# Attention and channel mix on one core: q stacks in two parts on SyncE, x asked for later, the second projection in idle banks

## The chip, the cores and the metric

One core of a Trainium2 chip runs the whole program. The metric is the device time of one execution in microseconds (us). TensorE is PE in the profile, with PEld for its weight loads; VectorE is DVE, ScalarE is ACT, GpSimd is POOL, SyncE is SP. SPq and ACTq rows are DMA issues on the queues of SyncE and ScalarE.

## The reference

```python
x = layernorm(x + attn(x)); x = layernorm(x + ffn(x))        # x: 1 x 4096 x 256, float32
# attn: 16 heads of 16, 4 groups of k and v, window of 128 keys, causal
scores = einsum('bghqd,bgkd->bghqk', q, k) / sqrt(16);  mask = (i - 128 >= j) | (i < j)
out = softmax(where(mask, -1e9, scores)) @ v;  return out @ Wo + bo
# ffn: x_prev is x one token earlier
r = sigmoid(xr @ W_r.T); k = square(relu(xk @ W_k.T)); return r * (k @ W_v.T)
```

## The kernel before

The 4096 tokens are 32 blocks of 128 (t), four blocks to a superblock (s, eight of them; j is the block's place in its superblock, 0 to 3). All queues are written out by hand: each engine has a function start() and a function step(s, j, ...), called once for each block, and engines meet at semaphores. A step works on several blocks at once: the row maxima of block t+1, the scores, exponentials and masks of block t, the product with v of block t-1, the output projection of t-2, the channel mix of t-3 and t-4, and the store of t-5.

Projections are made by superblock. Each of its three chunks (chunk 0 is k and v, chunks 1 and 2 are q) is projected in float32 by TensorE (`project_chunk`, L876), and split by ScalarE (`high_part`, L492, and `middle_part`, L503), VectorE (`rest_part`, L663) and GpSimd (`low_part`, L378) into three bf16 parts whose sum is the float32 value. Chunks 0 and 1 of superblock s+2 are made in step j=3 of s, chunk 2 in step j=0 of s+1. The parts are written to DRAM (`spill_k` L298, `spill_q` L292) and read back with the six combinations of parts stacked along partitions, 16 rows for each: `stack_k` (L311, L313) into ks, 80 KB each, and `stack_q` (L512) into qs. One superblock's q stack is six transfers of 256 KB, each to 16 partitions, and ks and qs have two buffers, by the superblock's parity (par).

`tile_q` (L680) on VectorE copies a block's queries from qs into q_tiles, two steps ahead of the block: in step j=2 of superblock s it takes the first block of s+1, in j=3 the second. The maxima's products (`max_scores`, L923 and L932) of the next step begin with it. VectorE reduces them (L688), and `turn_max` (L695 to L702) turns the maxima into rows, which SyncE sends to two rows of qs (`max_in`, L321, two transfers of 4 KB) for the score product of the next block (L949).

In the step, SyncE issues in this order: in j=0 `spill_k`, the wait for its landing, six `stack_k`, `max_in`, then `spill_q` twice; in j=1 `max_in`, `load_x(s+2)` (x_t and x_in, 512 KB each); in every step the store of block t-5 last. ScalarE issues the six `stack_q` of superblock s+1 in step j=1, between its exponentials 4 and 5. GpSimd adds bo to the four blocks of x of s+1 in step j=2 (`x_plus_bo`, L372).

In the start, superblock 0 is projected in three banks, superblock 1 in proj_ps alone, one chunk after the other, and its chunk 2 after the second group of block 0's maxima. ScalarE issues the whole q stack of superblock 0 there, and VectorE's first `tile_q` waits for all of it. VectorE waits on s_stack, which counts the six k and the six q transfers of a superblock together.

```python
                if j == 0:
                    dve.wait_ge(s_stack, s * STACKS + STACKS)
```

Of the kernel before, what the change touches and what calls it, by code (L numbers as in the profile page):

```python
# [32 lines left out]
WINDOW = 128  # L33
# [4 lines left out]
SB_BLKS = 4  # L38
# [16 lines left out]
def attention_channel_mix(nc, x_nat, x_feat, w_first, w_rest, out):  # L55
# [25 lines left out]
    with ExitStack() as ctx:  # L81
# [6 lines left out]
        def sem(name):  # L88
            return ctx.enter_context(nc.semaphore(name))
# [85 lines left out]
        s_spill_k = sem("s_spill_k")  # L175
        s_spill_q = sem("s_spill_q")
        s_stack = sem("s_stack")
        s_tiles = sem("s_tiles")
        s_maxsc = sem("s_maxsc")
        s_max = sem("s_max")  # L180
# [93 lines left out]
        def _(sp):  # L274
# [26 lines left out]
            def stack_k(s, par, rep):  # L301
                if rep == 0:

                    sp.wait_ge(s_spill_k, s * 16 + 16)
                    if later(s, 2):

                        sp.wait_ge(s_score, scored(s * SB_BLKS - SB_BLKS - 1, NSCORE - 1))
                    sp.nop(nofuse=True)
                src = k_dram[K_PART[rep]].rearrange("(g d) t -> d g t", d=DH)
                if not later(s, 1):  # L310
                    sp.dma_start(ks[rep * DH:(rep + 1) * DH, par, :, WINDOW:], src[:, :, 0:SB]).then_inc(s_stack, 16)  # L311
                else:
                    sp.dma_start(ks[rep * DH:(rep + 1) * DH, par],  # L313
                                 src[:, :, bass.ds(s * SB - WINDOW, WINDOW + SB)]).then_inc(s_stack, 16)

            def max_in(t, j, par):

# [11 lines left out]
            def start():  # L329
                load_x(0, 0)  # L330
                sp.dma_start(rest_w[:, :], w_rest).then_inc(s_restw, 16)
                load_x(1, 1)
                spill_k(0)
                for m in range(QCH):
                    spill_q(0, 0, m)
                for rep in range(NREP):
                    stack_k(0, 0, rep)
                max_in(0, 0, 0)

            def step(s, j, par, project, coming, maxima, scores):  # L340
                t = s * SB_BLKS + j

                if project and j == 0:
                    spill_k(s + 1)
                    for rep in range(NREP):
                        stack_k(s + 1, 1 - par, rep)
                if maxima:
                    max_in(t + 1, *at(j, par, 1))
                if project and j == 0:
                    spill_q(s + 1, 1 - par, 0)  # L350
                    spill_q(s + 1, 1 - par, 1)
                if coming and j == 1:
                    load_x(s + 2, par)
                if behind(t, j, scores, 5):
                    store(t - 5, (j - 5) % 2)

# [9 lines left out]
        def _(pool):  # L366
# [31 lines left out]
            def start():  # L398
# [22 lines left out]
                                            channel_multiplier=1).then_inc(s_const, 1)  # L421
                pool.wait_ge(s_const, 5 + 3 * HPG)
                pool.wait_ge(s_restw, 16)
                x_plus_bo(0, 0)
                for m in range(NCH):
                    low_part(0, m)
                x_plus_bo(1, 1)
                for m in range(NCH):
                    low_part(1, m)

            def step(s, j, par, project, coming, maxima, scores):
                t = s * SB_BLKS + j
# [50 lines left out]
        def _(act):  # L483
# [18 lines left out]
                act.wait_ge(s_rest, s * NCH + m + 1)  # L502
                nc.scalar.copy(parts[:, m, 1], rest[:, m]).then_inc(s_mid, 1)  # L503

            def stack_q(s, par, rep):
                if rep == 0:

                    act.wait_ge(s_spill_q, s * SPILLS + SPILLS)
                    if later(s, 2):

                        act.wait_ge(s_score, scored(s * SB_BLKS - SB_BLKS - 1, NSCORE - 1))
                act.dma_start(qs[rep * DH:(rep + 1) * DH, par].rearrange("d j (m x) g t -> d (j m) (x g t)", m=QCH),  # L512
                             q_dram[par, Q_PART[rep]].rearrange("j m (d y) t -> d (j m) (y t)", d=DH)
                             ).then_inc(s_stack, 16)

            def exps(t, i, buf):
                act.wait_ge(s_score, scored(t, i))
                if i <= 1 and later(t, 2):
# [4 lines left out]
            def start():  # L523
                act.dma_start(first[:, :], w_first).then_inc(s_first, 16)
                act.wait_ge(s_const, 1)
                nc.scalar.activation(warm[:, :], minus_half[:, :], ACT.Exp)
                act.wait_ge(s_first, 16)
                for m in range(NCH):
                    high_part(0, m, (proj_ps, max_ps[0], max_ps[1])[m])
                    if m:  # L530
                        middle_part(0, m - 1)
                middle_part(0, NCH - 1)
                high_part(1, 0)
                for rep in range(NREP):
                    stack_q(0, 0, rep)
                middle_part(1, 0)
                high_part(1, 1)
                middle_part(1, 1)
                high_part(1, 2)
                middle_part(1, 2)  # L540

            def step(s, j, par, project, coming, maxima, scores):
# [81 lines left out]
                    high_part(s + 1, 2)  # L624
                if scores and t:
                    exps(t, 4, j % 2)
                if project and j == 1:
                    for rep in range(NREP):
                        stack_q(s + 1, 1 - par, rep)
                if scores:  # L630
                    exps(t, 5, j % 2)
                if coming and j == 3:
# [21 lines left out]
        def _(dve):  # L654
# [21 lines left out]
            def tile_q(t, s, j, par):  # L676

                if j == 0:
                    dve.wait_ge(s_stack, s * STACKS + STACKS)
                nc.vector.tensor_copy(q_tiles[:, j % 2].rearrange("r n (h q) -> r n h q", q=SUB),  # L680
                                      qs[0:ROWS, par, j].rearrange("r h g (n q) -> r (g n) h q", q=SUB)
                                      ).then_inc(s_tiles, 1)
# [31 lines left out]
            def start():  # L714
# [14 lines left out]
                    nc.vector.tensor_copy(edge_mask[:, n], edge_f[:, :, :]).then_inc(s_masks, 1)  # L729
                nc.vector.tensor_copy(first_mask[:, :, :], first_f[:, :, :]).then_inc(s_masks, 1)  # L730

                rest_part(1, 0)
                rest_part(1, 1)
                tile_q(0, 0, 0, 0)
                tile_q(1, 0, 1, 0)
                for i in range(NMAXB):
                    tile_max(0, 0, i)
                turn_max(0, 0)
                rest_part(1, 2)
                val_copy(1, 1)  # L740

            def step(s, j, par, project, coming, maxima, scores):
                t = s * SB_BLKS + j
# [113 lines left out]
        def _(pe):  # L857
            def project_chunk(s, m, par, ps=None):

                if m == 0:  # L860
                    pe.wait_ge(s_xt[par], loaded(s, par))
                    if later(s, 1):

                        pe.wait_ge(s_val, s)
                    if later(s, 2):

                        pe.wait_ge(s_max, (s - 1) * SB_BLKS * NMAXB)
                elif ps is None:
                    pe.wait_ge(s_rest, s * NCH + m)
                    if m == 1:  # L870
                        pe.wait_ge(s_pcp, s + 1)
                    if m == 2 and later(s, 2):

                        pe.wait_ge(s_max, ((s - 1) * SB_BLKS + 2) * NMAXB)
# [5 lines left out]
            def v_turn(s):  # L880

                pe.wait_ge(s_pcp, s + 1)
                pe.wait_ge(s_rest, s * NCH + (NCH if later(s, 1) else 1))
                if later(s, 2):

                    pe.wait_ge(s_max, ((s - 1) * SB_BLKS + 3) * NMAXB)
# [82 lines left out]
            def start():  # L969
# [2 lines left out]
                    project_chunk(0, m, 0, (proj_ps, max_ps[0], max_ps[1])[m])  # L972
                pe.wait_ge(s_ident, 1)
                v_turn(0)
                for m in range(QCH):
                    project_chunk(1, m, 1)
                pe.wait_ge(s_zero, 5)
                pe.wait_ge(s_masks, 2 + TPB)
                for i in range(NMAXB):
                    max_scores(0, 0, 0, i)  # L980
                    if i == 1:
                        project_chunk(1, QCH, 1)
                v_turn(1)
                pe.wait_ge(s_restw, 16)

            def step(s, j, par, project, coming, maxima, scores):
# [168 lines left out]
```

## Time and profile before

| | |
|---|---|
| median of 3 runs | 492.97 us (490.83 to 494.72) |
| the profiled execution | 496.05 us, of which its span is 494.0 us |
| mean granted TensorE clock in it | 0.913 |
| busy: PE, DVE, ACT, POOL | 408.5, 340.5, 272.9, 287.1 us |
| DMA moved | 39.24 MB |

The span is from the first to the last instruction. Busy shares are of the whole span, over stretches with different limits. The granted clock is a share of 2.4 GHz: 1.0 is that level, 0.5 is 1.2 GHz.

### The profile page before, as it was taken

How to read it: one execution, taken by the hardware profiler on the slowest of the kernel's cores; microseconds unless marked ns; L12 is line 12 of the kernel's file. 1: busy time of each engine (PE TensorE's matmuls, PEld its weight loads, DVE VectorE, ACT ScalarE, POOL GpSimd, SP SyncE). 2: the span in 40 equal slices, each digit the busy share in tenths (PEclk: the TensorE clock that was granted, in tenths of full speed). 3: DMA queues.
4: the chain of work that ended last, by engine and by line, in shares of the span. 5: the costliest groups of instructions: out<-in, count | busy, mean ns of one | idle time of the engine just before them, and what ended most of it. 6: DMA issues, size and time to landing. Idle time of an engine off the chain costs nothing.

```text
span 494.0 us, 8282 instructions
## 1 busy us (share of the span) xinstructions
PE 408.5 (83%) x2494; PEld 252.1 (51%) x2494; DVE 340.5 (69%) x851; ACT 272.9 (55%) x566; POOL 287.1 (58%) x466
## 2 busy tenths in 40 slices
PE   5407686998799978998799888998699979999964
PEld 2104344565455645665455554665455646765542
DVE  5506653588677886688677875688677987996541
ACT  3301343665656764776477563776466566877521
POOL 5500343575747775676567684676557785787521
PEclk9857687999999998999899996999999998999965
DMA  7780583035902393146704391146703390000000
GB/s 297 138 100 7 115 168 49 10 81 88 182 12 58 77 189 47 37 107 108 129 13 89 77 187 17 38 106 105 131 13 70 86 118 12 23 14 23 12 21 21
DMA packets 50124, 39.24 MB, mean 79 GB/s; under 512 B 32929, under 2 KB 41633, under 8 KB 49953
## 3 DMA queue, kind: packets, MB, share of 16 engines
q1 hardware_dynamic: 43024, 25.74, 23.2%
q10 hardware_dynamic: 7056, 12.98, 16.9%
q8 instruction: 20, 0.33, 0.3%
q14 instruction: 24, 0.19, 0.2%
HBM read 26.38 MB, written 12.06 MB: 78 GB/s over the span
## 4 chain that ended last, share of the span: by engine, by line
PE 47%; DMA 24%; ACT 8%; DVE 6%; POOL 4%; issue 4%; ACTq 4%; SPq 1%; POOLq 0%; DVEq 0%
DMA qs<-q_parts 22%; PE proj_ps L876 8%; PE av_ps L963 7%; PE score_ps L949 6%; PE gen L997 5%; PE max_ps L932 4%; PE gen L1054 4%; ACTq L512 4%; PE gen L1043 4%; PE gen L1032 3%; ACT probs L521 3%; POOL probs L386 2%; PE max_ps L923 2%; DVE q_tiles L680 2%; ACT parts L492 2%
## 5 line engine op out<-in xcount | busy, mean ns | idle before, releaser
L386 POOL TENSOR_SCALAR_AFFINE_SELECT probs<-probs 128x512 f32<-128x512 f32 x252 | 165.8, 668 | 121.2 <-ACT probs L521 118.1
L521 ACT ACTIVATE probs<-score_ps 128x512 f32<-128x512 f32 x252 | 148.4, 598 | 112.1 <-PE score_ps L949 94.6
L949 PE MATMUL score_ps<-qs,ks 98*128 98x512 bf16 x252 | 100.8, 403 | 15.7 <-ACT probs L521 12.7
L688 DVE TENSOR_REDUCE neg_max<-max_ps 128x3 f32<-128x480 f32 x144 | 87.3, 631 | 18.9 <-PE max_ps L932 18.2
L963 PE MATMUL av_ps<-probs,vals 128*32 128x512 f32 x504 | 67.9, 613 | 0.9 <-POOL probs L386 0.8
L949 PEld LDWEIGHTS score_ps<-qs,ks 98*128 98x128 bf16 x252 | 25.0, 100 | 73.3 <-ACT probs L521 58.4
L393 POOL TENSOR_TENSOR rstd<-var,minus_half 128x1 f32<-128x1 f32 x64 | 35.7, 558 | 34.3 <-DVE var L712 33.7
L876 PE MATMUL proj_ps<-x_t,first 128*128 128x512 f32 x88 | 47.0, 660 | 10.0 <-DMA first<-w_first 5.4
L932 PE MATMUL max_ps<-ks,q_tiles 96*128 96x160 bf16 x416 | 53.3, 247 | 0.0
L1043 PE MATMUL gen<-mix,rest_w 128*128 128x128 f32 x256 | 38.5, 298 | 13.1 <-DVE mix L763 11.9
L680 DVE COPY q_tiles<-qs 96x2048 bf16<-96x2048 bf16 x32 | 25.8, 810 | 33.9 <-DMA qs<-q_parts 33.9
L923 PE MATMUL max_ps<-edge_mask,ident_b 128*128 128x192 bf16 x138 | 35.9, 260 | 15.7 <-DVE q_tiles L680 14.4
L378 POOL TENSOR_TENSOR parts<-rest,parts 128x512 bf16<-128x512 f32 x24 | 30.3, 1263 | 27.8 <-ACT parts L503 27.7
L1043 PEld LDWEIGHTS gen<-mix,rest_w 128*128 128x128 f32 x256 | 35.1, 206 | 19.2 <-DVE mix L763 14.3
L663 DVE SCALAR_TENSOR_TENSOR rest<-proj_ps,first,parts 128x512 f32<-128x512 f32 x22 | 16.5, 748 | 40.7 <-ACT parts L492 37.6
L763 DVE SCALAR_TENSOR_TENSOR mix<-diff,first,x_t 128x128 f32<-128x128 f32 x128 | 43.9, 386 | 0.0
L932 PEld LDWEIGHTS max_ps<-ks,q_tiles 96*128 96x128 bf16 x416 | 38.7, 104 | 7.9 <-issue 2.5
L997 PE MATMUL gen<-rest_w,act_k 128*128 128x256 f32 x128 | 38.5, 427 | 1.9 <-ACT act_k L592 1.8
L1032 PE MATMUL gen<-rest_w,mix 128*128 128x256 f32 x128 | 35.4, 400 | 3.0 <-DVE mix L763 3.0
L492 ACT ACTIVATE parts<-proj_ps,first 128x512 bf16<-128x512 f32 x22 | 15.1, 687 | 40.0 <-PE proj_ps L876 40.0
L1054 PE MATMUL gen<-rest_w,att_c 128*128 128x256 f32 x128 | 35.4, 401 | 0.0
L876 PEld LDWEIGHTS proj_ps<-x_t,first 128*128 128x128 f32 x88 | 16.9, 208 | 28.6 <-issue 19.0
(74 smaller groups left out, 636.1 us busy)
## 6 DMA issues: line engine op xcount, KB each, us to landing
qs<-q_parts ACTq DMA_DIRECT2D x48, 256.0 KB, 11.1
q_parts<-parts SPq DMA_DIRECT2D x48, 128.0 KB, 2.2
x_t<-x_feat SPq DMA_DIRECT2D x8, 512.0 KB, 9.3
x_in<-x_nat SPq DMA_DIRECT2D x8, 512.0 KB, 12.5
out<-out_t SPq DMA_DIRECT2D x32, 128.0 KB, 2.0
ks<-k_parts SPq DMA_DIRECT2D x42, 80.0 KB, 3.0
k_parts<-parts SPq DMA_DIRECT2D x8, 192.0 KB, 2.8
rest_w<-w_rest SPq DMA_DIRECT2D x1, 1152.0 KB, 7.7
```

The costliest lines, as they stand in the source:

```text
L386: nc.gpsimd.affine_select(out=v, in_=v, compare_op=ALU.is_ge if i % 2 else ALU.is_gt, fill=0.0, base=0, pattern=[[0, HPG], [sign, BLK]], c ...
L521: nc.scalar.activation(probs[:, buf, i], score_ps[i % 2][:, :], ACT.Exp, scale=SCALE).then_inc(s_exp, 1)
L688: nc.vector.tensor_reduce(neg_max[:, TPB * i:TPB * i + n], max_bank(t, j, i)[:, 0:n * TILE_KEYS].rearrange("p (n k) -> p n k", k=TILE_KEYS ...
L876: ins = nc.tensor.matmul((ps or proj_ps)[:, 0:SB], wqkv[:, c, m * P:(m + 1) * P], x_t[:, par, c], start=(c == 0), stop=(c == DC - 1))
L923: nc.tensor.matmul(edges, ident_b[:, :], edge_mask[:, 0:len(tiles)], start=True, stop=False, skip_group_check=True)
L932: ins = nc.tensor.matmul(dst, q_tiles[:, j % 2, tile], ks[0:ROWS, par, g, k0:k0 + TILE_KEYS], start=False, stop=(k == len(tiles) - 1), ski ...
L949: nc.tensor.matmul(score_ps[i % 2][:, :].rearrange("p (h q) -> p h q", q=BLK), ks[0:ROWS + MPARTS, par, g, k0:k0 + BLK], qs[0:ROWS + MPART ...
L963: ins = nc.tensor.matmul(av_ps[g * VCOL:(g + 1) * VCOL, :], vals[:, pk, jk, g, :], probs[:, j % 2, 2 * g + half], start=(half == 0 or not ...
L997: ins = nc.tensor.matmul(gen0[:, 0:D], act_k[:, c], w_t[:, 2, c], start=(c == 0), stop=(c == DC - 1))
L1032: ins = nc.tensor.matmul(gen0[:, 0:D], mix[:, 0, c], w_t[:, 0, c], start=(c == 0), stop=(c == DC - 1))
L1043: ins = nc.tensor.matmul(gen0[:, o * BLK:(o + 1) * BLK], w_t[:, 1, c, o * P:(o + 1) * P], mix[:, 1, c], start=(c == 0), stop=(c == DC - 1))
L1054: ins = nc.tensor.matmul(gen1[:, 0:D], att_c[:, c], wo[:, c], start=(c == 0), stop=(c == DC - 1))
```

## The change

The q stack is issued by SyncE in two parts: the first block of a superblock (six transfers of 64 KB) in step j=1, counted with the k stacks on a new semaphore s_stack0, and the other three blocks (six of 192 KB) in step j=2, counted on s_stack, for which VectorE waits in its `tile_q` of j=1's block. ScalarE issues the stack no more, except the first block's of superblock 0 in the start; there SyncE issues the other three blocks when the first block's and the k stacks have landed, ahead of `max_in(0)`. x of superblock s+3 is asked for in step j=3 (x of superblock 2 in j=1 of superblock 0) instead of x of s+2 in j=1. In the start the three chunks of superblock 1 go to gen0, gen1 and av_ps, all of them ahead of the maxima of block 0, and the second `tile_q` stands behind the maxima. GpSimd's two `x_plus_bo` of the start stand later, among the `low_part`s.

```diff
             def stack_k(s, par, rep):
 ...
-                    sp.dma_start(ks[...]).then_inc(s_stack, 16)
+                    sp.dma_start(ks[...]).then_inc(s_stack0, 16)
+            def stack_q(s, par, first, done):
+                lo, hi = (0, 1) if first else (1, SB_BLKS)
+                sp.wait_ge(s_spill_q, s * SPILLS + SPILLS)
+                if later(s, 2):
+                    sp.wait_ge(s_score, scored(s * SB_BLKS - SB_BLKS - 1, NSCORE - 1))
+                for rep in range(NREP):
+                    sp.dma_start(qs[rep * DH:(rep + 1) * DH, par, lo:hi]..., q_dram[par, Q_PART[rep], lo:hi]...
+                                 ).then_inc(done, 16)
 # SyncE, start
                     stack_k(0, 0, rep)
+                sp.wait_ge(s_stack0, STACKS)
+                stack_q(0, 0, False, s_stack)
                 max_in(0, 0, 0)
 # SyncE, step
-                if coming and j == 1:
-                    load_x(s + 2, par)
+                if project and j == 1:
+                    stack_q(s + 1, 1 - par, True, s_stack0)
+                    if s == 0:
+                        load_x(2, 0)
+                if project and j == 2:
+                    stack_q(s + 1, 1 - par, False, s_stack)
+                if j == 3 and s + 3 < NSB:
+                    load_x(s + 3, 1 - par)
 # GpSimd, start
-                x_plus_bo(0, 0)
                 for m in range(NCH):
                     low_part(0, m)
+                x_plus_bo(0, 0)
+                low_part(1, 0)
                 x_plus_bo(1, 1)
-                for m in range(NCH):
-                    low_part(1, m)
+                low_part(1, 1)
+                low_part(1, 2)
 # ScalarE, start
-                high_part(1, 0)
+                high_part(1, 0, gen0)
+                high_part(1, 1, gen1)
+                middle_part(1, 0)
+                high_part(1, 2, av_ps)
+                act.wait_ge(s_spill_q, SPILLS)
                 for rep in range(NREP):
-                    stack_q(0, 0, rep)
-                middle_part(1, 0)
-                high_part(1, 1)
+                    act.dma_start(qs[rep * DH:(rep + 1) * DH, 0, 0]...).then_inc(s_stack0, 16)
                 middle_part(1, 1)
-                high_part(1, 2)
 # ScalarE, step
-                if project and j == 1:
-                    for rep in range(NREP):
-                        stack_q(s + 1, 1 - par, rep)
 # VectorE
                 if j == 0:
-                    dve.wait_ge(s_stack, s * STACKS + STACKS)
+                    dve.wait_ge(s_stack0, s * STACKS + STACKS)
+                elif j == 1:
+                    dve.wait_ge(s_stack, (s + 1) * STACKS // 2)
 # VectorE, start
-                rest_part(1, 0)
-                rest_part(1, 1)
+                rest_part(1, 0, gen0)
+                rest_part(1, 1, gen1)
+                rest_part(1, 2, av_ps)
+                val_copy(1, 1)
                 tile_q(0, 0, 0, 0)
-                tile_q(1, 0, 1, 0)
                 for i in range(NMAXB):
                     tile_max(0, 0, i)
                 turn_max(0, 0)
-                rest_part(1, 2)
-                val_copy(1, 1)
+                tile_q(1, 0, 1, 0)
 # TensorE, start
-                for m in range(QCH):
-                    project_chunk(1, m, 1)
+                for m in range(NCH):
+                    project_chunk(1, m, 1, (gen0, gen1, av_ps)[m])
+                v_turn(1)
                 for i in range(NMAXB):
                     max_scores(0, 0, 0, i)
-                    if i == 1:
-                        project_chunk(1, QCH, 1)
-                v_turn(1)
```

`project_chunk` waits for the values' copy (s_val) only from superblock 2 on, and `v_turn(1)` waits for s_val of superblock 0 instead of the rest parts.

## Rows read from the trace of the kernel before

**Rows 1.** The page's chain that ended last, share of the span by line.

```profile
DMA qs<-q_parts 22%; PE proj_ps L876 8%; PE av_ps L963 7%; PE score_ps L949 6%; PE gen L997 5%; PE max_ps L932 4%; PE gen L1054 4%; ACTq L512 4%; PE gen L1043 4%; PE gen L1032 3%; ACT probs L521 3%; POOL probs L386 2%; PE max_ps L923 2%; DVE q_tiles L680 2%; ACT parts L492 2%
```

**Rows 2.** Waits of the whole span: engine and line, releaser, us, times, longest.

```profile
DVE q_tiles L680 <- DMA qs<-q_parts: 33.9, 7, 12.2
...
ACT probs L521 <- issue: 17.5, 7, 2.6
...
PE max_ps L923 <- DVE q_tiles L680: 14.4, 7, 4.0
```

**Rows 3.** Timeline of SyncE's queue: start, duration, line, transfer, count.

```profile
131.14 1.12 SPq L321 DMA_DIRECT2D qs<-max_rows  x2
...
144.17 1.11 SPq L321 DMA_DIRECT2D qs<-max_rows  x2
...
225.66 1.12 SPq L321 DMA_DIRECT2D qs<-max_rows  x2
...
239.15 1.12 SPq L321 DMA_DIRECT2D qs<-max_rows  x2
...
252.50 1.11 SPq L321 DMA_DIRECT2D qs<-max_rows  x2
...
259.43 0.63 SPq L298 DMA_DIRECT2D k_parts<-parts  x1
262.29 2.67 SPq L313 DMA_DIRECT2D ks<-k_parts  x6
267.25 1.12 SPq L321 DMA_DIRECT2D qs<-max_rows  x2
...
293.35 1.12 SPq L321 DMA_DIRECT2D qs<-max_rows  x2
...
309.55 1.11 SPq L321 DMA_DIRECT2D qs<-max_rows  x2
```

**Rows 4.** Timeline, end of step j=1 of superblock 3; brackets: idle before, releaser.

```profile
226.06 2.92 ACTq L512 DMA_DIRECT2D qs<-q_parts  x6
...
229.03 0.60 ACT L521 ACTIVATE probs<-score_ps 128x512 f32<-128x512 f32 x1 [2.42 <-issue]
...
229.68 0.39 PE L949 MATMUL score_ps<-qs,ks 98*128 98x512 bf16 x1 [1.51 <-ACT probs L521]
```

**Rows 5.** Timeline, step j=2 of superblock 3 and the step behind it.

```profile
240.22 1.66 PE L1043 MATMUL gen<-mix,rest_w 128*128 128x128 f32 x8 [1.99 <-DVE mix L763]
...
244.28 0.69 DVE L680 COPY q_tiles<-qs 96x2048 bf16<-96x2048 bf16 x1 [3.50 <-DMA qs<-q_parts]
...
245.03 0.26 PE L923 MATMUL max_ps<-edge_mask,ident_b 128*128 128x192 bf16 x1 [1.45 <-DVE q_tiles L680]
```

**Rows 6.** Timeline of VectorE, step j=3 of superblock 3.

```profile
256.30 0.68 DVE L680 COPY q_tiles<-qs 96x2048 bf16<-96x2048 bf16 x1
...
260.09 0.75 DVE L663 SCALAR_TENSOR_TENSOR rest<-proj_ps,first,parts 128x512 f32<-128x512 f32 x1 [1.41 <-ACT parts L492]
```

**Rows 7.** Windows: stretch, length, busy (count) of PE, PEld, DVE, ACT, POOL, clock, DMA share, GB/s.

```profile
6.00:12.00 6.00, 6.00 (x12) 2.48 (x11) 2.52 (x10) 2.46 (x4) 2.46 (x3) 1.00 0.86 357
...
22.00:37.00 15.00, 0.80 (x2) 0.00 (x0) 0.76 (x2) 1.82 (x3) 2.31 (x2) 0.61 0.89 109
...
238.00:244.30 6.30, 3.59 (x16) 2.42 (x14) 2.74 (x7) 3.17 (x8) 3.29 (x5) 0.73 0.88 135
```

**Rows 8.** Line L321 (maxima's rows), those issued in 251 to 254: from issue to landing.

```profile
DMA to landing us min/median/max: 1.7/1.7/1.8
```

**Rows 9.** Line L321, those issued in 238 to 242: from issue to landing.

```profile
DMA to landing us min/median/max: 4.7/4.8/5.0
```

**Rows 10.** The chain that ended last in order of time: start, us, what.

```profile
22.27 14.70 DMA qs<-q_parts
```

**Rows 11.** Timeline of TensorE, scores of block 1.

```profile
57.00 1.03 PE L949 MATMUL score_ps<-qs,ks 98*128 98x512 bf16 x2 [2.16 <-DMA qs<-max_rows]
```

**Rows 12.** Timeline of TensorE, first maxima of block 1.

```profile
47.60 0.25 PE L923 MATMUL max_ps<-edge_mask,ident_b 128*128 128x192 bf16 x1
```

More of the change, by code:

```diff
@@ L177, in attention_channel_mix @@
         s_stack = sem("s_stack")
+        s_stack0 = sem("s_stack0")
         s_tiles = sem("s_tiles")
@@ L310, in stack_k @@
                 if not later(s, 1):
-                    sp.dma_start(ks[rep * DH:(rep + 1) * DH, par, :, WINDOW:], src[:, :, 0:SB]).then_inc(s_stack, 16)
+                    sp.dma_start(ks[rep * DH:(rep + 1) * DH, par, :, WINDOW:], src[:, :, 0:SB]).then_inc(s_stack0, 16)
                 else:
                     sp.dma_start(ks[rep * DH:(rep + 1) * DH, par],
-                                 src[:, :, bass.ds(s * SB - WINDOW, WINDOW + SB)]).then_inc(s_stack, 16)
+                                 src[:, :, bass.ds(s * SB - WINDOW, WINDOW + SB)]).then_inc(s_stack0, 16)
+            def stack_q(s, par, first, done):
[4 more added lines that the diff above has]
+                for rep in range(NREP):
+                    sp.dma_start(qs[rep * DH:(rep + 1) * DH, par, lo:hi].rearrange("d j (m x) g t -> d (j m) (x g t)", m=QCH),
+                                 q_dram[par, Q_PART[rep], lo:hi].rearrange("j m (d y) t -> d (j m) (y t)", d=DH)
+                                 ).then_inc(done, 16)
             def max_in(t, j, par):
@@ L503, in middle_part @@
                 nc.scalar.copy(parts[:, m, 1], rest[:, m]).then_inc(s_mid, 1)
[L505 to L514, printed above, removed]
             def exps(t, i, buf):
@@ L532, in start @@
                 middle_part(0, NCH - 1)
-                high_part(1, 0)
+                high_part(1, 0, gen0)
[3 more added lines that the diff above has]
+                act.wait_ge(s_spill_q, SPILLS)
                 for rep in range(NREP):
-                    stack_q(0, 0, rep)
-                middle_part(1, 0)
-                high_part(1, 1)
+                    act.dma_start(qs[rep * DH:(rep + 1) * DH, 0, 0].rearrange("d (m x) g t -> d m (x g t)", m=QCH),
+                                  q_dram[0, Q_PART[rep], 0].rearrange("m (d y) t -> d m (y t)", d=DH)
+                                  ).then_inc(s_stack0, 16)
                 middle_part(1, 1)
-                high_part(1, 2)
                 middle_part(1, 2)
@@ L861, in project_chunk @@
                     pe.wait_ge(s_xt[par], loaded(s, par))
-                    if later(s, 1):
+                    if later(s, 2):
                         pe.wait_ge(s_val, s)
@@ L882, in v_turn @@
                 pe.wait_ge(s_pcp, s + 1)
-                pe.wait_ge(s_rest, s * NCH + (NCH if later(s, 1) else 1))
+                if s == 1:
+                    pe.wait_ge(s_val, 1)
+                else:
+                    pe.wait_ge(s_rest, s * NCH + (NCH if later(s, 1) else 1))
                 if later(s, 2):
```

## The prediction

> **What bounds the kernel now.** I read the page's chain first: the longest single item in it is no compute but the q stack's DMA, with 22% of the span, and ScalarE's issue of it holds another 4% [rows 1]. A chain follows the last releaser only, so its share is no price. The waits give that: VectorE stood still for the stack 33.9 us in seven times, one of them 12.2 us long; TensorE stood 14.4 us in seven times before the first maxima product of a step, for the copy that VectorE made after that wait; and ScalarE had seven waits with no releaser, 2.6 us the longest, 17.5 in all [rows 2]. Seven is the number of q stacks that a step asks for.
>
> Then SyncE's timeline, as a ruler: each `max_in` ends the maxima of a step, so the distance of two of them is a step's length. Call them M0 to M3 by j. In superblock 3 M1 to M2 is 13.49 us, M2 to M3 13.35, M3 to the next M0 14.75 [rows 3]. The stretches with the stack in them are as long as the one with two projection chunks. Two timelines show why. At the end of j=1 the queue of ScalarE holds six DMA issues (2.92 us); the exponential behind them starts 2.42 us late, and TensorE, whose score product waits for that bank, loses 1.51 [rows 4]. In j=2 VectorE is ready for `tile_q` at 240.78 (244.28 less 3.50), the stack lands at 244.28, and TensorE idles 1.45 before L923 [rows 5]. Ahead of that there is another idle time of 1.99 us, for VectorE's mix [rows 5], in the step in which GpSimd has `x_plus_bo`. The change touches neither. Around it the granted clock is 0.73 on average, part of the stretch at 1.2 GHz: TensorE had idled twice before it fell [rows 7].
>
> **The change part by part.**
>
> *ScalarE's issues go.* Six superblocks (1 to 6) have the picture of rows 4; TensorE gets back at most 1.51 us in each. VectorE's own work ahead of the next reduction fills about 0.1 of it by my estimate, so 1.4: 6 x 1.4 = 8.4 us. Ends: 0 (VectorE is next and has no slack) and 9.1.
>
> *SyncE's twelve issues.* They cost it two times about 3 us (2.92 on ScalarE [rows 4]) in j=1 and j=2, behind `max_in`; behind them on SyncE stand the store and the next `max_in`, 10 us later. Nothing, therefore, unless a wait in them blocks: the spills' landing is due long before M1, and the score of the block before as well.
>
> *The first block's stack.* Issued from M1 + 1.2 on, 0.39 MB. The rate has a row: from 22 to 37 us in the start the q stack is nearly alone, at 109 GB/s [rows 7]. 3.6 us plus 1.7 for a small transfer to land [rows 8], and no faster than its six issues: landed at M1 + 7. `tile_q` wants it at M2 + 1.6, which is M1 + 13. The wait of rows 5 goes whole: TensorE's 14.4 us [rows 2] less nothing. 4.0 of that is in superblock 0.
>
> *The other three blocks.* 1.18 MB, asked for at M2 + 1.2. At 109 GB/s 10.8 us plus 1.7 is 12.5; by the stack of superblock 3, which had x beside it and took 18.2 us from first issue to landing (226.06 to 244.28) [rows 4, 5], three quarters are 13.7. I take 13: landed at M2 + 14.2 (13.7 to 14.9). M3 will be at M2 + 10.5 (below, with the clock). So it lands at M3 + 3.7. Who wants it is `tile_q` in j=3, at 256.30, M3 + 3.8, held until then by the projection [rows 6]. A tie, with a cushion: VectorE idles 1.41 us a little later [rows 6], and the maxima of the next step come behind chunk 1. I cost it at nothing, and 0.5 us more for each us beyond M3 + 5.2. In superblock 6, with no chunks, it is wanted 2 us earlier; there it costs what the old wait did at most (1.5).
>
> *x in j=3.* Issued at M3 + 1.2 behind the stack in SyncE's ring, data from M3 + 2.7 on; 1.05 MB at the start's 357 GB/s [rows 7] is 3 us, at half of that 6: done at M3 + 6 to 9. `spill_k` is issued at M3 + 6.9 and `max_in` at M3 + 14.75, with the landing of k (2.9 us) and six k stacks (2.67) between, so that SyncE is free 2.3 us before M0 (264.96) [rows 3]. So it costs nothing up to a delay of 2.3 us. x is wanted four steps later.
>
> *The clock.* With idle of 1.99 alone instead of 1.51, 1.99 and 1.45 in some 16 us, it should fall less. What it cost: M2 to M3 was 13.03 in superblock 1, 13.35 in 3, 16.20 in 4 [rows 3]. Without the wait and at full clock it lies between 9.85 (13.35 less VectorE's whole 3.50) and 11.9 (less TensorE's 1.45 alone); I take 10.4, since part of TensorE's work there ran at the lower level. In superblock 3 that leaves 13.35 - 1.45 - 10.4 = 1.5 for the clock, in 4, with a mean wait of 10.4 / 6 = 1.7, 4.1, and in 1 perhaps nothing, the whole 2.6 being wait. Superblocks 2, 5 and 6 as 3: 4 x 1.5 + 4.1 = 10 at most. As the idle time for the mix stays, I take half, 5. Ends 0 and 10.
>
> *The start.* The six issues of the q stack end with one at 22.27, and it lands at 36.97 [rows 10]; each takes 0.5 (2.92 / 6), so the first was at about 20, when the spills had landed. After the change ScalarE has three operations of about 0.7 ahead of it (`high_part(1, 1)` waits for the same spills), so 22.3; with 64 KB each all six land by 28 (22.3 + 3.6 + 1.7). Then `tile_q` and block 0's maxima run, from 28.7 to about 34, while SyncE sends the other three blocks: 28 + 13 = 41.2. The second `tile_q` waits for them and the maxima of block 1 start at 41.9, against 47.60 now [rows 12]. Then a second gain: now the scores of block 1 start at 57.00, the last 2.16 us in wait for their maxima's rows, which lie behind the k stacks of superblock 1 [rows 11]. Those k stacks now start behind the three blocks, at 41.5, and are through by 49. Scores at 49: 8 us. Ends: 5.5 (only the first gain) and 9.5. That the second projection needs no bank between is hidden behind the stack, either way.
>
> *Superblock 0* has ScalarE's issues too (1.5 as in rows 4, with 0.4 more for the lower clock) and at most 1 us of clock behind its wait of 4.0.
>
> *Sum:* start 8; superblock 0 2 + 4 + 1 = 7; issues 8.4; waits 14.4 - 4.0 = 10.4; clock 5. 38.8 us. The profiled execution took 496.05, so 457. It was 3.1 above the median of the runs; that is one fall of the clock, about the 4.1 of superblock 4, whose return the sum holds in part. I take 458 for the median.
>
> **The rivals.**
>
> *A: the clock doesn't recover.* The idle time for the mix stays and stands just ahead of each fall (240.22 in rows 5). Then the 5 and the 1 of superblock 0 go, and some of the falls that cost 1.5 move to other places: 464. Against it: superblock 1 had all three idle times and no loss. For it: it takes no more than rows 5 show.
>
> *B: the three blocks land late.* SyncE's ring now carries everything. If the big part runs at 90 GB/s it lands at M3 + 6; VectorE waits 2.3, TensorE 1 in each of six: 464; with the second `tile_q` of the start as late, 467. Beside the clock's loss, 473. For it: the 18.2 us above, and the tie. Against: with x no longer beside it, it should rather go faster.
>
> *C: the maxima's rows behind the bulk, slower than before.* Now the bulk is in ScalarE's ring, and `max_in` of j=2 lands 4.7 us after its issue with bulk and x in flight, 1.7 with none [rows 9, 8]. After the change `max_in` of j=3 stands behind 1.18 MB in one ring. The scores that need it can't start before M3 + 6.9, when the step's projection parts are done and the next step begins (259.43) [rows 3]. With the stack landed at M3 + 3.7 there are some 3 us to spare. The price beyond: at 65 GB/s the three blocks take 18.2 + 1.7 us and land at M3 + 10.6, `tile_q` is 7 us late, x ends at M3 + 14 at the earliest, and the landing of k and the k stacks behind it (5.5 us and more) push `max_in` of j=0 from M3 + 14.75 to 20 and later: 6 to 7 us in each of seven superblocks, 46, less the 38.8 gained: 503. It decides from 5.5 us each (38.8 / 7), about 70 GB/s. The 109 GB/s, measured over 15 us, is against it.
> The Trainium skill's page "DMA: Bandwidth & Descriptors", section "Queues, rings and completion order", says that each DMA engine takes turns between the rings of the issuing engines and works off one ring in order. By that rule `max_in` can no longer overtake the bulk, as in C; rows 8 and 9 agree that it is slowed even in its own ring, where x stood ahead of it, and no row shows it behind the stack itself. By the rule alone it lands at M3 + 4.5 and the sum stays as it is.
>
> *D: the wait was a symptom.* Were VectorE next without slack in j=1 and j=2 (busy with reductions that wait for nothing), only the start and half of the steps' gain would show: 8 + 7 + 10 = 25, so 471. Against: VectorE idled before the reductions in both places.
>
> **How the numbers follow.** Forecast (454 to 462) 0.5; A 0.2; B 0.13; D 0.08; better than the forecast, all of the clock given back (448 to 453) 0.05; C 0.04. The range reaches from full clock to B with the clock lost: 447 to 474, which leaves C and the worst of B and D out. Faster by over 1% 0.95, within 1% 0.02, slower 0.03; 1% is about what a measurement here can tell.
>
> **What the profile of the changed kernel would show.** ACTq issues only in the start; no idle of ScalarE for "issue" in j=1, and M1 to M2 about 12.1. `tile_q` in j=2 without a wait, M2 to M3 10.4 to 10.7; in j=3 a wait for qs of 0 to 1 us, 2 in superblock 6. Six issues of 192 KB landing 12.5 to 13.7 us after the first. Maxima of block 1 at 42, scores at 49. Mean clock above 0.913, up to 0.95. Wrong would be: a wait for qs of over 2 us in j=3, `max_in` of j=3 or j=0 among TensorE's releasers, or M3 to M0 longer than 14.75.

## The result, and the profile after

The changed kernel takes 454.22 us, median of four runs (452.07 to 456.63), against 492.33 (490.83 to 494.72): 0.922 of the time before, with a 95% interval of 0.916 to 0.928. The profiled execution took 452.07 us with a span of 450.3 and a mean granted clock of 0.945. Some executions are slower than the others of their kernel, one of experiment 4 by far (782 us, with matmuls up to twice as long); medians here are of all executions, ratios of the faster ones alone, so that a ratio can differ a little from that of its two medians.

The page's chain, and the waits of the whole span (engine and line, releaser: us, times, longest), which answer to [rows 1, 2]:

```profile
PE av_ps L980 11%; PE score_ps L966 9%; PE proj_ps L890 8%; PE gen L1058 6%; PE gen L1012 6%; PE max_ps L949 6%; PE gen L1069 5%; PE gen L1047 4%; DVE neg_max L702 4%; DVE max_parts L709 3%; DVE q_tiles L694 3%; PE max_ps L940 3%; DMA qs<-q_parts 2%; ACT parts L515 2%; DVE mix L777 2%
```

```profile
PE gen L1058 <- DVE mix L777: 15.4, 6, 2.6
...
PE max_ps L940 <- DVE q_tiles L694: 5.4, 1, 5.4
DVE q_tiles L694 <- DMA qs<-q_parts: 5.4, 2, 3.3
```

VectorE's wait for the stack fell from 33.9 us in seven times to 5.4 in two, both in the start; TensorE's one wait of 5.4 at L940 is in the start. ScalarE's waits without a releaser are gone. What grew is TensorE's wait for VectorE's mix, 1.99 us before [rows 5], now 2.6 for the longest.

SyncE's queue in superblock 3, the ruler (start, duration, line, transfer, count), which answers to [rows 3]:

```profile
198.90 1.12 SPq L334 DMA_DIRECT2D qs<-max_rows  x2
200.11 2.87 SPq L325 DMA_DIRECT2D qs<-q_parts  x6
...
211.60 1.12 SPq L334 DMA_DIRECT2D qs<-max_rows  x2
212.82 2.90 SPq L325 DMA_DIRECT2D qs<-q_parts  x6
...
223.32 1.12 SPq L334 DMA_DIRECT2D qs<-max_rows  x2
...
230.25 0.64 SPq L299 DMA_DIRECT2D k_parts<-parts  x1
233.11 2.67 SPq L314 DMA_DIRECT2D ks<-k_parts  x6
238.07 1.12 SPq L334 DMA_DIRECT2D qs<-max_rows  x2
```

M1 to M2 is 12.70 us (13.49 before), M2 to M3 11.72 (13.35), M3 to M0 14.75 as before. Read so over the whole span, the 43.7 us between the two profiles lie like this: 10.2 up to M0 of superblock 0 (53.29 to 43.05); 11.1 from there to its M3 (36.20 to 25.11), and 0.7 in the step behind; 5.0 in the six stretches M1 to M2 of superblocks 1 to 6; 14.0 in their six M2 to M3; and 2.7 behind the last `max_in` (M2 of superblock 7), where no q stack is: there the mean clock was 0.86 instead of 0.77. The windows of that last stretch, before and after (length, busy and count of PE, PEld, DVE, ACT, POOL, granted clock, DMA share, GB/s):

```profile
447.75:494.00 46.25, 33.61 (x159) 20.99 (x157) 19.83 (x66) 19.93 (x46) 18.84 (x35) 0.77 0.06 21
```

```profile
406.74:450.30 43.56, 30.46 (x159) 18.94 (x157) 19.82 (x66) 19.81 (x46) 18.84 (x35) 0.86 0.07 22
```

The same count of instructions, VectorE and ScalarE busy for the same time, TensorE 3.15 us less: clock alone, and no work of the change.

M2 to M3 of superblocks 3 and 5 of the changed kernel, as windows:

```profile
211.60:223.32 11.72, 10.64 (x65) 7.03 (x66) 9.35 (x27) 5.68 (x12) 6.13 (x12) 0.85 0.75 113
314.88:324.93 10.05, 9.00 (x65) 5.76 (x66) 9.39 (x27) 5.75 (x12) 6.05 (x12) 1.00 0.81 112
```

Five of the six stretches are like the first (11.52 to 11.73), one like the second. So a fall of the clock costs 1.67 us here, and it came five times. Before, five of the six were below 1.00 too (superblocks 2 to 6, 0.68 to 0.88).

### The profile page after: what moved, and what is told of

It is laid out like the page before. It is cut to its first block, busy times and chain, and to the rows that moved or that the text cites. A ratio compares the mean times of both kernels' runs of the same rounds, so it can differ in the third digit from the quotient of the medians.

```text
span 450.3 us, 8335 instructions
## 1 busy us (share of the span) xinstructions
PE 396.8 (88%) x2494; PEld 247.7 (55%) x2494; DVE 344.1 (76%) x851; ACT 273.0 (61%) x566; POOL 291.1 (65%) x466
## 4 chain that ended last, share of the span: by engine, by line
PE 63%; DVE 18%; ACT 6%; issue 5%; DMA 4%; POOL 1%; SPq 1%; ACTq 0%; DVEq 0%; POOLq 0%
PE av_ps L980 11%; PE score_ps L966 9%; PE proj_ps L890 8%; PE gen L1058 6%; PE gen L1012 6%; PE max_ps L949 6%; PE gen L1069 5%; PE gen L1047 4%; DVE neg_max L702 4%; DVE max_parts L709 3%; DVE q_tiles L694 3%; PE max_ps L940 3%; DMA qs<-q_parts 2%; ACT parts L515 2%; DVE mix L777 2%
## 5 line engine op out<-in xcount | busy, mean ns | idle before, releaser
L408 POOL TENSOR_SCALAR_AFFINE_SELECT probs<-probs 128x512 f32<-128x512 f32 x252 | 168.2, 678 | 108.7 <-ACT probs L533 106.4
L966 PE MATMUL score_ps<-qs,ks 98*128 98x512 bf16 x252 | 99.8, 398 | 2.2 <-ACT probs L533 1.4
L890 PE MATMUL proj_ps<-x_t,first 128*128 128x512 f32 x76 | 38.3, 628 | 5.5 <-DMA first<-w_first 5.5
L675 DVE SCALAR_TENSOR_TENSOR rest<-proj_ps,first,parts 128x512 f32<-128x512 f32 x19 | 14.3, 751 | 35.9 <-ACT parts L515 32.5
L940 PE MATMUL max_ps<-edge_mask,ident_b 128*128 128x192 bf16 x138 | 35.4, 257 | 6.5 <-DVE q_tiles L694 5.4
L1012 PE MATMUL gen<-rest_w,act_k 128*128 128x256 f32 x128 | 36.0, 405 | 2.1 <-ACT act_k L607 2.0
L1047 PE MATMUL gen<-rest_w,mix 128*128 128x256 f32 x128 | 34.3, 390 | 3.0 <-DVE mix L777 3.0
L1069 PE MATMUL gen<-rest_w,att_c 128*128 128x256 f32 x128 | 32.9, 379 | 0.0
L694 DVE COPY q_tiles<-qs 96x2048 bf16<-96x2048 bf16 x32 | 27.1, 847 | 5.4 <-DMA qs<-q_parts 5.4
L601 ACT ACTIVATE relu_k<-gen 128x256 f32<-128x256 f32 x32 | 12.7, 397 | 29.6 <-PE gen L1058 29.6
L580 ACT ACTIVATE x<-y,shift,rstd 128x256 f32<-128x256 f32 x32 | 19.2, 599 | 17.2 <-POOL shift L417 16.3
```

Of the source, the lines that this page charges most:

```text
L408: nc.gpsimd.affine_select(out=v, in_=v, compare_op=ALU.is_ge if i % 2 else ALU.is_gt, fill=0.0, base=0, pattern=[[0, HPG], [sign, BLK]], c ...
L890: ins = nc.tensor.matmul((ps or proj_ps)[:, 0:SB], wqkv[:, c, m * P:(m + 1) * P], x_t[:, par, c], start=(c == 0), stop=(c == DC - 1))
L966: nc.tensor.matmul(score_ps[i % 2][:, :].rearrange("p (h q) -> p h q", q=BLK), ks[0:ROWS + MPARTS, par, g, k0:k0 + BLK], qs[0:ROWS + MPART ...
L1012: ins = nc.tensor.matmul(gen0[:, 0:D], act_k[:, c], w_t[:, 2, c], start=(c == 0), stop=(c == DC - 1))
L1047: ins = nc.tensor.matmul(gen0[:, 0:D], mix[:, 0, c], w_t[:, 0, c], start=(c == 0), stop=(c == DC - 1))
L1069: ins = nc.tensor.matmul(gen1[:, 0:D], att_c[:, c], wo[:, c], start=(c == 0), stop=(c == DC - 1))
```

## The experiments

Times are medians; the ratio is to the kernel before, timed beside them on the same chip (496.11 us for e1, e2, e3 and e6, 494.13 for e4, e5, e7 and e8, 493.65 for e9 to e12), with its 95% interval. Distances M0 to M3 come from SyncE's queue in each profile.

**1. ScalarE issues the parts.** As the changed kernel, but both parts in ScalarE's queue.

```diff
 # ScalarE, step, behind exps(t, 4)
+                if project and j == 1:
+                    stack_q(s + 1, 1 - par, True, s_stack0)
+                if project and j == 2:
+                    stack_q(s + 1, 1 - par, False, s_stack)
```

> The changed kernel, with the twelve q issues of a superblock on ScalarE again (six of 64 KB in j=1, six of 192 KB in j=2, at the old place). Theory (ScalarE's issue time is its own term): ScalarE stands about 2.5 us twice in a superblock, TensorE loses up to 1.5 each; in j=1 some of it is absorbed by the wait behind x_plus_bo. M1 to M2 13.3 (12.70 in the changed kernel), M2 to M3 12.5 (11.72 with a fall of the clock); six to seven times 1.5 to 2.2, so 464 to 468. Rival (the stall by issues only hides another wait): 454 to 457.

Measured: 492.74 us, 0.994 (0.989 to 1.000): nearly the whole gain gone, beyond either theory. M1 to M2 is 13.46, as before the change. But M2 to M3 is 14.1 to 16.1. TensorE, step behind M2 (229.95) of superblock 3, the big part having been issued from 228.47 on, and the landing of the maxima's rows issued at 229.95:

```profile
228.81 2.37 ACTq L532 DMA_DIRECT2D qs<-q_parts  x5
...
229.95 1.11 SPq L334 DMA_DIRECT2D qs<-max_rows  x2
...
238.51 0.61 PE L978 MATMUL score_ps<-qs,ks 98*128 98x512 bf16 x1 [3.53 <-DMA qs<-max_rows]
```

```profile
DMA to landing us min/median/max: 6.8/7.4/8.0
```

8 KB wait 7 us in SyncE's ring, with nothing ahead of them in it, where 1.18 MB were issued from 1.5 us earlier on in ScalarE's. The scores wait, and from 232 to 245 us the mean clock is 0.74. The start of this kernel is the changed one, which alone is worth 13 us (experiment 5); so the split in ScalarE's hands made the steps slower than they were before. In the changed kernel the same rows land in 1.7 to 1.8 us, since the big part is issued behind them.

**2. Only the order in time.** Two kernels tell the ring from the moment. In the first ScalarE issues the big part, but behind exps(t, 7), after the rows; in the second SyncE issues it, but ahead of them.

```diff
 # e9: ScalarE, step
                     exps(t, 7, j % 2)
+                if project and j == 2:
+                    stack_q(s + 1, 1 - par, False, s_stack)
 # e10: SyncE, step, ahead of max_in
+                if project and j == 2:
+                    sp.wait_ge(s_exp, scored(t, 4))
+                    stack_q(s + 1, 1 - par, False, s_stack)
```

> As the run with ScalarE's issues in j=1 and j=2, but the big part is issued behind the last exponential of j=2, after the maxima's rows have gone (there it was issued 1.4 us ahead of them, and they landed 6.8 to 8.0 us after their issue, in the other ring; TensorE waited 3.5 us for them). Theory (what matters is that the bulk starts behind the rows, not whose ring it is in): rows of j=2 land in 1.7 to 2 us, no wait of the score product for them; the two stalls of ScalarE stay, 0.8 and 1.5: M2 to M3 13.2 instead of 14.1 to 16.1, 468 to 472 in all. Rival (ScalarE's issue time is what costs): 485 to 493.

> The changed kernel, SyncE issuing everything, with the big part ahead of the maxima's rows in j=2: SyncE waits for exponential 4 of that step, the moment at which ScalarE issued it, then sends the big part, then the rows. Theory (order in time): the rows land 8 us and more after they are ready, TensorE waits 3.5 to 5 us for them in each of six superblocks, and SyncE's issue puts 1.5 us on top: M2 to M3 15 to 16.5, 476 to 485. Rival (the rows overtake nothing only across rings, and in one ring they go in turn at once): as the changed kernel, 454 to 458.

Measured: 457.54 us, 0.926 (0.922 to 0.929), and 496.88 us, 0.998 (0.993 to 1.003). The waits of the second, and the landing of its rows issued at 230.17:

```profile
PE score_ps L967 <- DMA qs<-max_rows: 28.4, 7, 8.2
```

```profile
DMA to landing us min/median/max: 7.8/7.9/7.9
```

Some 35 to 40 us hang on whether 1.18 MB go 1.5 to 2.8 us ahead of 8 KB or behind them, and little on the issuing engine. The two kernels don't split this cleanly: e9 also moves ScalarE's stall behind the last exponential, and e10 holds SyncE up, so that M1 to M2 is 14.0 instead of 12.7 (8 us in six superblocks). But e10 has no stall of ScalarE and is as slow as e1, so the order carries most of it. It came out slower than my 476 to 485; my 468 to 472 for the first was too high, for a reason that its windows show (M2 to M3 of superblock 3):

```profile
214.89:225.00 10.11, 9.04 (x65) 5.76 (x66) 9.46 (x27) 5.56 (x12) 6.83 (x13) 1.00 0.65 110
```

With ScalarE's issues in the way M1 to M2 is 13.44 to 13.46 in five superblocks and 14.98 in one, but the clock doesn't fall behind it (1.00 in all six windows): M2 to M3 is 10.11 to 10.17 in five and 10.75 in one. M1 to M3 of superblock 3 is 23.56 us, 0.86 less than in the changed kernel. What it loses is in superblock 0, whose M0 to M3 is 29.83 against 25.11.

**3. Whole stack, x, and where each lies.** The whole stack in one piece by SyncE in j=1; and the changed kernel with x of s+2 in j=1 again.

```diff
 # e2: SyncE, step
                 if project and j == 1:
-                    stack_q(s + 1, 1 - par, True, s_stack0)
+                    stack_q(s + 1, 1 - par, None, s_stack0)      # None: all four blocks
-                if project and j == 2:
-                    stack_q(s + 1, 1 - par, False, s_stack)
 # e3: SyncE, step
-                    if s == 0:
-                        load_x(2, 0)
-                if j == 3 and s + 3 < NSB:
-                    load_x(s + 3, 1 - par)
+                if coming and j == 1:
+                    load_x(s + 2, par)
```

> The changed kernel, with the whole q stack (six of 256 KB) issued by SyncE in j=1, nothing in j=2, x in j=3. Landing from M1 + 1.2 at the 130 GB/s seen in the changed kernel: 12.1 + 1.7, so M1 + 15. Theory (the split is what removes the wait): tile_q in j=2 wants it at M2 + 1.6, M1 + 14.3, so a wait of 0.7 in VectorE and none in TensorE: 454 to 456. max_in of j=2 stands behind it, lands at M2 + 2.3 and is wanted 6 us later: nothing. In superblock 0, whose M1 to M2 is 8.4, the wait is 5 us, so 458 in all. Rival (x beside the stack, not its size, made it late): the same, so this run prices the split. If ring order hurts: above 462.

> The changed kernel, with x of s+2 asked for in j=1 behind the first block's stack, as before the change. Theory (x is gone from the ring before the big part starts): x lands at M1 + 11, the big part isn't touched: 452 to 456. Rival (x in flight slows the stacks): big part late, a wait for qs in j=3, 458 or more.

Measured: 465.98 us, 0.939 (0.932 to 0.946), and 454.42 us, 0.917 (0.911 to 0.923). Without the split superblock 0 has an M2 to M3 of 17.06 (9.35 in the changed kernel), since its M1 to M2 is only 9.2 and the stack can't be there; in the later ones M2 to M3 is 11.5 to 12.3, with VectorE waiting 0.6 to 2.0 us for the stack. My 458 for it was too low. By the two ratios the split is worth 8 us, by the medians 12, by the profiles 13.4: 8.8 of these lie in superblock 0, 2.7 in the six later M2 to M3, and 3.0 behind the last `max_in`, at a clock of 0.77 against 0.86. The maxima's rows of superblock 0, issued at M2 while the whole stack is still in SyncE's ring, landed after 9.5 to 9.7 us. With the split it is all the same where x goes.

**4. x alone, on the kernel before.** The reverse: nothing changed but x, asked for in j=3.

```diff
 # SyncE, step, kernel before
-                if coming and j == 1:
-                    load_x(s + 2, par)
+                if j == 1 and s == 0:
+                    load_x(2, 0)
+                if j == 3 and s + 3 < NSB:
+                    load_x(s + 3, 1 - par)
```

> The kernel before, with nothing changed but x asked for in j=3. Theory (x beside the stack costs part of VectorE's wait): the stack lands 14.6 to 15 us after its first issue as in superblock 6, instead of 18.2; VectorE's wait in j=2 falls from 3.5 to 0.3, TensorE's 1.45 goes and with it part of the clock's falls: 482 to 486. Rival (the stack's own rate is the limit, the 13 us that I took for the big part): wait stays above 2 us, 489 to 493.

> The kernel before with x asked for in j=3 once more, for a profile of it. The time was 471 to 476, far below the 482 to 486 that the wait of VectorE alone would give. Theory (the rows again: without x the stack of j=1 is through at M2 + 1 to 2, so TensorE's wait goes and the clock falls less): VectorE's wait in j=2 below 0.5 us, M2 to M3 10.1 to 11.7, M1 to M2 13.5 as before, sum 471 to 477. Rival (a gain in the start or in superblock 0): M3 of superblock 0 more than 5 us earlier, M2 to M3 of the later ones above 12.

Measured: 474.77 us, 0.963 (0.954 to 0.972), and again 473.80, 0.958 (0.955 to 0.961). The waits of the second:

```profile
ACT probs L523 <- issue: 17.3, 7, 2.5
...
DVE q_tiles L682 <- DMA qs<-q_parts: 15.0, 3, 11.2
```

The first is far below my 482 to 486; the second meets the 471 to 477 that I then gave. In it VectorE's waits for the stack in superblocks 1 to 6 are gone but for less than a microsecond, with the stack still in one piece and ScalarE's issues still there. M2 to M3 is 10.06 to 10.07 in five superblocks, 10.29 in one, at full clock, where before it was 11.7 to 16.2: 21.8 us in six stretches, more than the 14.0 of the whole change. So x out of the way of the stack gives by itself about half of what the change gives. In the steady superblocks each of the two moves takes the wait away, x later (e11) and the split with x in j=1 (e3). In e3 SyncE issues as well; the whole stack in SyncE's ring, ahead of x in j=1, was not run, so that for e3 the split and the order in that ring are not told apart.

**5. Start and steps apart, and the banks.** The change's steps on the start of before; the change's start on the steps of before; and the changed kernel with the second projection in proj_ps alone, chunk 2 behind the second group of maxima, each as the hunks of the change's diff undone.

```diff
 # e7, the banks: TensorE, start
-                for m in range(NCH):
-                    project_chunk(1, m, 1, (gen0, gen1, av_ps)[m])
-                v_turn(1)
+                for m in range(QCH):
+                    project_chunk(1, m, 1)
```

> The steps of the changed kernel (q stack in two parts on SyncE, x in j=3) with the start of the kernel before (whole stack on ScalarE, second projection in one bank). By the profiles the start gave 10.2 us up to M0 of superblock 0: 464. By the prediction's terms the start gives 8: 462. Rival (the start's gain is a shift that a later wait takes back): 454 to 456.

> The start of the changed kernel with the steps of the kernel before (whole stack on ScalarE in j=1, x in j=1). By the terms of the prediction 492 - 8 = 484, by the profiles 492 - 10 = 482. Rival (taken back by the stack of superblock 1, which is asked for by a chain of its own): 488 to 492.

> The changed kernel, with the second projection in proj_ps alone again, its chunk 2 after the second group of block 0's maxima. Theory (hidden behind the stack of the start): ScalarE's issues start 2 us earlier, the chunk of 3.6 us goes between the maxima while VectorE has the big part to wait for: 453 to 456. Rival (the banks carry part of the start's gain, through SyncE's k stack, which needs only chunk 0, or through the maxima's end): 457 to 460.

Measured: 465.82 us, 0.946 (0.937 to 0.954); 479.28, 0.973 (0.965 to 0.981); 457.65, 0.929 (0.919 to 0.939). Steps and start add up: 5.4% and 2.7% are the 7.8% within the intervals, so nothing takes the start's gain back. M0 of superblock 0 is at 52.5, 43.1 and 44.7. The last is 1.6 later than in the changed kernel, but in the nine profiles whose start is wholly that of the changed kernel M0 lies at 41.2 to 44.2, so neither this nor the time tells the banks from nothing.

**6. The addition of bo.** The changed kernel, with GpSimd adding bo to one block in each step instead of four in j=2; and this one with ScalarE issuing the 64 KB transfers of j=1.

```diff
 # e6: GpSimd, step
-                if ahead and j == 2:
-                    x_plus_bo(s + 1, 1 - par)
+                if ahead:
+                    x_plus_bo_block(s + 1, 1 - par, j)    # x_bo[:, par, j] = x_in[:, par, j] + bo_b
 # e12: ScalarE, step, behind exps(t, 4), on top of e6
+                if project and j == 1:
+                    stack_q(s + 1, 1 - par, True, s_stack0)
```

> The changed kernel, with GpSimd's addition of bo to four blocks in j=2 (2.4 us in one) cut into one block in each step. Theory (the remaining loss of j=2 is VectorE held by that addition, 2.58 us of TensorE idle, and the fall of the clock behind it, 1.67): M1 to M2 from 12.70 to 10.5, M2 to M3 from 11.7 to 10.1, 3.5 to 4 us in each of six superblocks, 431 to 436. Rival 1 (the clock falls anyway): 439 to 442. Rival 2 (four short additions hold VectorE as long in all, at other places): 450 to 455.

> The version with bo added by block (434.5), with the six transfers of 64 KB of j=1 issued by ScalarE again, the big part by SyncE. Theory (in the changed kernel part of ScalarE's 1.5 us was given back as a longer wait behind x_plus_bo; with that wait gone the stall counts in full): M1 to M2 from 10.55 to 12.0, six or seven times 1.45: 443 to 445. Rival (0.8 each, as between the changed kernel and the one with ScalarE's issues): 439 to 440.

Measured: 434.48 us, 0.878 (0.873 to 0.882), and 445.52, 0.901 (0.896 to 0.905). The first is the fastest version of this study, 4.3% below the changed kernel. In the changed kernel (first fence) the small cast of 16 values stands as long as GpSimd's addition, and TensorE behind it; in this version (second fence) the mix is 0.32 us late, and M2 to M3 runs at full clock:

```profile
208.31 2.36 POOL L394 TENSOR_TENSOR x_bo<-x_in,rest_w 128x1024 f32<-128x1024 f32 x1
...
208.42 2.29 DVE L709 CAST max_parts<-neg_max 128x16 bf16<-128x16 f32 x1
...
212.68 1.97 PE L1058 MATMUL gen<-mix,rest_w 128*128 128x128 f32 x8 [2.58 <-DVE mix L777]
```

```profile
200.96 0.73 POOL L402 TENSOR_TENSOR x_bo<-x_in,rest_w 128x256 f32<-128x256 f32 x1
...
203.07 1.16 PE L1067 MATMUL gen<-mix,rest_w 128*128 128x128 f32 x8 [0.32 <-DVE mix L786]
```

```profile
202.26:212.71 10.45, 10.13 (x70) 5.97 (x69) 9.86 (x27) 6.86 (x15) 7.50 (x14) 1.00 0.83 115
```

M1 to M2 is 10.55 (12.70), M2 to M3 10.45 to 10.74 (11.72). The second kernel has M1 to M2 of 11.35 in four superblocks: ScalarE's issue costs 0.8 there too, so rival 0.8 is right for the stretch and my 1.45 wrong, though the whole came out at 445.5, above both. Its 11 us in all are more than 6 x 0.8: 3.1 are in superblock 0 (11.89 against 8.77, at a clock of 0.86 against 1.00) and 2.8 in one superblock with 14.15, where ScalarE stood 3.42 us instead of 2.4 and the window's clock was 0.88. One stretch of e9 looks alike (14.98); why ScalarE stood longer there I don't know.

## Why the prediction was right, point by point

Forecast 458, measured 454.2, within the range. The sum was made for the profile of 496.05 and came to 38.8; that profile fell by 44.0 (to 452.07), the medians by 38.1. That the number came so near is in part luck. Against the 43.7 of the profiles the terms miss both ways: the start by +2.2, superblock 0 and the step behind it by +4.8, the last stretch by +2.7, ScalarE's issues by -3.4, waits and clock in M2 to M3 by -1.4. And the kernel before was profiled in an execution slower than any of its four timed ones (496.05 against 494.72 at most), the changed one in the fastest of its own. By its steps:

- **The wait for the stack** (10.4 in superblocks 1 to 6, 4.0 in superblock 0): it is gone, and about right in size. The reading was not: I counted seven waits for seven stacks, but one of VectorE's is that of the start (12.2), one is in superblock 0, and five are in superblocks 1 to 5, behind which TensorE stood 10.0 us; superblock 6 has none. And it was right for the wrong half of a reason: I gave the gain to the split. Experiment 4 shows that asking for x later, which I looked at only as a cost, and put at nothing, takes the steady wait away alone, and experiment 3 that the split, issued by SyncE, does so too. The hint was in the trace: superblock 6 is the one without x, and the one without the wait.
- **The big part's landing** (M2 + 14.2, a tie with `tile_q`): mis-sized, M2 + 11.5 measured, 0.2 us before M3. The six transfers of superblock 3 took 10.3 us from first issue to landing (the last, issued at 215.3, took 7.8), against my 12.5 to 13.7. Two windows of that stretch have 127 and 136 GB/s, all DMA counted, where I used the start's 109. The cushion was there and wasn't needed; rival B fell with it.
- **ScalarE's issues** (1.4 each, 8.4): this term was mis-sized. M1 to M2 gave 0.8 each, 5.0 in all. More of the 1.51 is taken up elsewhere than the 0.1 that I estimated; not by the wait behind `x_plus_bo`, which in e12 is short (TensorE stands 0.3 us for the mix) and where the 0.8 is the same. What takes it up is not shown. Experiments 1, 9 and 12 show 13.46 against 12.68, 13.45, and 11.35 against 10.55: 0.8 each time.
- **The clock** (5 of 10): the term came out at 14.0 - 10.4 = 3.6 for M2 to M3, plus 2.7 in the last stretch, which I had not looked at. The latter is not clearly the change's: e4, with the same steps, took 45.94 us there at 0.78, hardly less than the kernel before. Rival A was right in its mechanism: the idle time for the mix stayed, and the clock fell in five of six superblocks, as often as before, though never for so long as in superblock 4 before. Worse, the change made that idle time longer. Where TensorE's idle ahead was 1.99 us and the stack wasn't late (e9, e11), all twelve stretches took 10.06 to 10.75; where it was 2.58 and the stack wasn't late (changed kernel, e3, e4, e7), 20 of 24 took 11.5 to 13.1. But 1.99 doesn't rule a fall out. Superblock 6 of the kernel before had it, with no late stack, and ran M2 to M3 in 11.71 at 0.85:

```profile
407.04 1.26 PE L1043 MATMUL gen<-mix,rest_w 128*128 128x128 f32 x8 [1.99 <-DVE mix L763]
```

```profile
405.97:417.68 11.71, 10.64 (x67) 7.26 (x68) 9.36 (x27) 5.82 (x13) 6.75 (x13) 0.85 0.05 13
```

With ScalarE's issue gone TensorE comes to the mix earlier and waits for it longer. So in the steady superblocks moving the issue to SyncE gave 0.8, and most of the stretches behind took 1.67 more than at full clock; what it is worth is small. That the longer idle makes the falls likelier is argued from these counts, not shown; e6, where the idle is 0.32 and no stretch M2 to M3 shows a fall, fits it. What else decides them is open.
- **The start** (8): 10.2 up to M0. The second `tile_q` came at 37.19, not 41.2: the big part was issued at 26.5, not 28, and took 10.7 us, not 13. The scores of block 1 started at 46.05, not 49. That the banks add nothing is not refuted (experiment 5).
- **Superblock 0** (7): 11.1. M1 to M2 fell by 4.7, not 2, M2 to M3 by 5.7, where I had 5. ScalarE's stall costs more here: M1 to M2 is 2.3 longer in e9 than in the changed kernel, 3.1 longer in e12 than in e6, there with a lower clock. That it is because few steps are under way is my guess.
- **Rival C** (the rows behind the bulk): its mechanism is real and large, and I had it at the wrong place. I looked for it in one ring. Experiments 1 and 2 show that it acts across rings just as well, and that the changed kernel escapes it since SyncE issues the big part behind `max_in` of j=2 and the part is through before the one of j=3. Had the parts been issued by ScalarE at the old place in the step, the change would have brought 3 us of 38, ten less than its start alone (e5). Nothing in my sum priced that. The Trainium skill's page "DMA: Bandwidth & Descriptors", section "Queues, rings and completion order", says that each DMA engine takes turns between rings by packets; by that rule alone the rows in a ring of their own should have slipped past the bulk. The 7.4 us of experiment 1 speak against using the rule so. Which resource they wait for, no run tells.

## What to carry to other kernels

A small transfer on which the next products hang is best issued ahead of a bulk transfer, or when that is through: here 8 KB behind 1.18 MB landed 5 to 6 us later than alone, in the same ring and in the other. Look at what else is in flight before a transfer is cut up: here moving the neighbour (x) alone gave 4.2%, all of the change's steps 5.4%. And a stall that is taken away ahead of a second stall can move TensorE's idle time there (1.99 to 2.58 us for the mix); here it was the last one whose removal gave most, 20 us in e6.

## What the runs showed of the hardware

- 8 KB in SyncE's ring landed 6.8 to 8.0 us after their issue with 1.18 MB issued from 1.5 us earlier on in ScalarE's ring (e1), 7.8 to 7.9 with them from 2.8 us earlier on in the same ring (e10), 1.7 to 1.8 ahead of the bulk (changed kernel, e9).
- A VectorE cast of 128x16 took 2.29 us beside a GpSimd addition of 128x1024 that ran 2.36, and 0.18 without it (changed kernel).
- In the changed kernel the same work (65 matmuls, M2 to M3) took 10.05 us at clock 1.00 and 11.72 at 0.85.
- With six transfers to 16 partitions each in flight, all DMA moved 109 GB/s in the start before (22 to 37 us), 128 in the start of the changed kernel (27 to 37 us) and 127 to 136 in its steps.
